# FFN norms of an attention and FFN megakernel: squares added up on VectorE in fp32, fewer statistic matmuls, and the closing 1/sqrt by Ln and Exp

## The reference

```python
def attn(X):                                     # layer 0, attention
    q, k, v = X@Wq.T + bq, X@Wk.T + bk, X@Wv.T + bv
    s = where(j > i, -inf, einsum('bie,bje->bij', q, k) / sqrt(E))
    return softmax(s, axis=-2) @ v
def ffn(x):                                      # three blocks
    h = x
    for blk in range(3):
        y = qlora_linear(h, 2*blk)               # w = q/7.5 - 1, times scale; plus a rank-32 term and a bias
        y = (y - mean(y)) * rsqrt(var(y) + 1e-5) * gamma + beta
        y = gelu(y)
        h = qlora_linear(y, 2*blk + 1) + h
    return h
x = layernorm(X + attn(X))
out = layernorm(x + ffn(x))
```

## Time and profile before

| | us |
|---|---|
| median of 3 runs | 1446.7 (1445.36 to 1462.48) |
| the profiled execution | 1443.28 |
| its span, slowest core (5) | 1441.7 (cores: 1429.3 to 1441.7) |
| TensorE busy | 1339.1 (93%) |
| VectorE busy | 698.4 (48%) |
| ScalarE busy | 750.5 (52%) |
| GpSimd busy | 424.5 (29%) |
| table loads on ScalarE | 48 of 1.283 each |

### The profile page before, as it was taken

The page is one execution under the profiler, slowest core; times in us unless marked ns, Lnnn a source line. Parts: engine busy times, 40 slices in busy tenths (PEclk is TensorE's granted clock), DMA queues, the critical chain, the costliest instruction groups (busy, mean ns, idle before and its releaser), DMA issues.

```text
span 1441.7 us, 21149 instructions; the slowest of 8 cores (1429.3 to 1441.7 us)
## 1 busy us (share of the span) xinstructions
PE 1339.1 (93%) x6724; PEld 620.1 (43%) x6724; DVE 698.4 (48%) x1474; ACT 750.5 (52%) x1104; POOL 424.5 (29%) x308
## 2 busy tenths in 40 slices
PE   6979999969899999888999999999989999999994
PEld 2434444434344444443444444445534444444552
DVE  1225555433344354416464365468634624736774
ACT  0135226653213356422784686576668748847741
POOL 4022353786623256654000019100100000650010
PEclk9988999989999999989999999999999999999998
DMA  9956545686855343485011035215641010550022
GB/s 137 217 164 201 172 146 139 198 239 204 282 177 203 117 147 131 167 292 224 11 59 46 14 104 169 78 32 190 222 143 58 2 59 1 182 169 1 30 103 103
DMA packets 70699, 192.17 MB, mean 133 GB/s; under 512 B 5696, under 2 KB 16192, under 8 KB 67520
## 3 DMA queue, kind: packets, MB, share of 16 engines
q1 hardware_dynamic: 48192, 133.40, 28.5%
q0 software_dynamic: 22400, 57.42, 14.3%
HBM read 158.03 MB, written 46.14 MB: 142 GB/s over the span
## 4 chain that ended last, share of the span: by engine, by line
PE 79%; DVE 5%; POOL 5%; issue 4%; ACT 3%; DMA 2%; another core or an unknown queue 1%; DVEq 0%; SPq 0%; ACTq 0%; POOLq 0%
PE ps L212 79%; ACT POOLT L216 3%; DVE POOLT L220 2%; POOL POOLT L612 2%; POOL POOLT L652 2%; DMA POOLT<-wq 1%; POOL POOLT L102 1%; DVE SM L994 1%; DMA POOLT<-bv_h 1%; DVE SM L229 1%; DVE POOLT L226 0%; POOL POOLT L394 0%; DVEq L108 0%; DVE POOLT L721 0%
## 5 line engine op out<-in xcount | busy, mean ns | idle before, releaser
L212 PE MATMUL ps<-POOLT 128*128 128x512 bf16 (+2 forms) x5600 | 1262.0, 378 | 30.7 <-DMA POOLT<-lb_h 8.7
L212 PEld LDWEIGHTS ps<-POOLT 128*128 128x128 bf16 (+1 forms) x5600 | 540.2, 99 | 685.1 <-issue 113.0
L216 ACT ACTIVATE POOLT<-ps,SM 128x512 bf16<-128x512 f32 (+4 forms) x396 | 262.6, 683 | 258.7 <-PE ps L212 156.5
L220 DVE TENSOR_TENSOR POOLT<-POOLT 128x512 bf16<-128x512 bf16 (+1 forms) x448 | 254.4, 604 | 211.9 <-ACT POOLT L216 191.6
L216 ACT ACTIVATE POOLT<-POOLT 128x512 bf16<-128x512 f32 (+4 forms) x234 | 175.8, 762 | 228.0 <-DMA POOLT<-qw_t 83.6
L220 DVE TENSOR_TENSOR POOLT<-ps,POOLT 128x512 bf16<-128x512 f32 (+1 forms) x176 | 117.0, 688 | 177.0 <-PE ps L212 151.9
L952 POOL TENSOR_TENSOR POOLT<-POOLT 128x512 f32<-128x512 f32 x64 | 89.6, 1424 | 373.8 <-DMA POOLT<-x1s 366.2
L394 POOL TENSOR_TENSOR POOLT<-POOLT 128x1024 f32<-128x1024 f32 x48 | 112.7, 2348 | 275.2 <-DMA POOLT<-sc_t 131.5
L216 ACT ACTIVATE POOLT<-POOLT,CF 128x512 bf16<-128x512 bf16 x192 | 154.3, 808 | 26.4 <-DVE POOLT L220 25.6
L212 PE MATMUL ps<-POOLT,CB 128*128 128x512 bf16 x320 | 116.5, 394 | 47.6 <-ACT POOLT L216 38.3
L216 ACT ACTIVATE POOLT<-POOLT,SM 128x512 bf16<-128x512 f32 (+2 forms) x120 | 110.0, 918 | 78.3 <-DVE SM L223 43.1
(11 more groups left out here) (53 smaller groups left out, 303.8 us busy)
## 6 DMA issues: line engine op xcount, KB each, us to landing
POOLT<-qw_t SPq DMA_DIRECT2D x48, 512.0 KB, 4.2
POOLT<-sc_t SPq DMA_DIRECT2D x48, 512.0 KB, 5.5
POOLT<-weffs SPq DMA_DIRECT2D x24, 1024.0 KB, 7.8
POOLT<-xt SPq DMA_DIRECT2D x16, 1024.0 KB, 10.6
x1s<-POOLT POOLq DMA_DIRECT2D x16, 1024.0 KB, 5.4
POOLT<-x1s SPq DMA_DIRECT2D x8, 2048.0 KB, 10.9
POOLT<-x1s SPq DMA_DIRECT2D x64, 256.0 KB, 3.2
out<-POOLT POOLq DMA_DIRECT2D x28, 512.0 KB, 4.1
```

Source lines behind the costliest of these rows:

```text
L212: return pe.put(lambda e: e.matmul(out, lhsT, rhs, start=start, stop=stop), *after, sig=sig)
L216: return act.put(lambda e: e.activation(out, in_, func, bias=bias, scale=scale, accum_out=acc), *after)
L220: return dve.put(lambda e: e.tensor_tensor(out, a, b, op), *after)
```

## The change

In y1 a chunk is still squared on VectorE, but into fp32, and the squares of a norm are added up there in fp32; only the last addition writes bf16, and one statistic matmul takes that sum (blocks 0 and 1). In the last block sums of two chunks are taken, so four statistic matmuls a norm. `add_square` replaces the square and the call of `after_groups(3, ...)`; it uses `after_groups(2, ...)`. The rates of `pre` in y1 go from 0.75 to 0.5. Ln and Exp on ScalarE with two waits replace the first 12 operations of a closing. Buffers are laid out anew for this.

```diff
+F_RS = (A_P2, A_MU, A_RS, A_SQ)
+F_TMP = (A_P2 + 512, A_P2 + 1024)
+F_SQ = A_P2 + 1536
+F_ACC = (A_LORA, A_LORA + 512)
...
+        def add_square(t, n, o, ty, stat_mm):
+            i = cnt["acc"] % 2
+            per = 8 if n < 2 else 2
+            k = o % per
+            tmp = FTMP[o % 2]
+            if k == 0:
+                sums[i] = v_tt(FACC[i], FY[t][o], FY[t][o], ALU.mult, ty, p_att)
+                return
+            ts = v_tt(tmp, FY[t][o], FY[t][o], ALU.mult, ty, p_att)
+            if k < per - 1:
+                sums[i] = v_tt(FACC[i], FACC[i], tmp, ALU.add, ts, sums[i])
+                return
+            q = cnt["sq"] % 3
+            cnt["sq"] += 1
+            cnt["acc"] += 1
+            tq = v_tt(FSQ[q], FACC[i], tmp, ALU.add, ts, sums[i], fsq_free[q])
+            after_groups(2, lambda: stat_mm(o, q, tq))
...
             for o in range(EC):
-                pre(0.75, 0.75)
+                pre(0.5, 0.5)
...
-                q = cnt["sq"] % 5
-                cnt["sq"] += 1
-                tq = v_tt(FSQ[q], FY[t][o], FY[t][o], ALU.mult, ty, fsq_free[q])
+                add_square(t, n, o, ty, stat_mm)
                 post()
-                after_groups(3, lambda o=o, q=q, tq=tq: stat_mm(o, q, tq))
...
-                ve, y, a, c2, nm = (two(x) for x in (28, 30, 32, 34, 36))
-                t1 = v_ts1(ve, var, EPS, ALU.add, *tb)
-                yi, vi = smi[:, fo + 30:fo + 30 + np_], smi[:, fo + 28:fo + 28 + np_]
-                t1 = v_ts1(yi, vi, 1, ALU.logical_shift_right, t1)
-                t1 = v_ts(yi, yi, -1, 0x5f3759df, ALU.mult, ALU.add, t1)
-                for _ in range(3):
-                    t1 = v_stt(a, y, -0.5, y, ALU.mult, ALU.mult, t1)
-                    t1 = v_tt(c2, a, ve, ALU.mult, t1)
-                    t1 = v_stt(y, c2, 1.5, y, ALU.add, ALU.mult, t1)
+                y, nm = two(30), two(36)
+                t1 = a_act(y, var, AF.Ln, *tb, bias=col(S_EPS))
+                t1 = a_act(y, y, AF.Exp, t1, scale=-0.5)
                 t1 = v_stt(nm, mean, -1.0, y, ALU.mult, ALU.mult, t1)
```

More of the change, by code:

```diff
@@ L702, in build_program @@
         FRS = [f32v(a, 512) for a in F_RS]
-        FSQ = [b16v(F_SQ + s * 256, 512) for s in range(5)]
+        FSQ = [b16v(F_SQ + s * 256, 512) for s in range(3)]
+        FACC = [f32v(a, 512) for a in F_ACC]
+        FTMP = [f32v(a, 512) for a in F_TMP]
         FXR = [f32v(F_XR + s * 512, 512) for s in range(4)]
@@ L833, in build_program @@
         fy_free[2], fy_free[3] = (p_att,), (p_att,)
-        frs_free = [(p_att,)] * 4
-        fsq_free = [p_att] * 5
+        frs_free = [(p_att,), None, None, None]
+        fsq_free = [p_att] * 3
         act_att = (act.sem, act.n)
-        cnt = {"sq": 0, "rs": 0, "xr": 0, "out": 0, "fo": 0}
+        cnt = {"sq": 0, "rs": 0, "xr": 0, "out": 0, "fo": 0, "acc": 0}
+        g0 = [0]
         finals = []
@@ L858, in post @@
                 gel_now.pop(0)()
+        sums = [None, None]
+        def add_square(t, n, o, ty, stat_mm):
[15 more added lines that the diff above has]
+            after_groups(2, lambda: stat_mm(o, q, tq))
         def y1(t, n):
@@ L866, in stat_mm @@
             def stat_mm(o, q, tok):
-                if o == 0:
+                if sb[0] is None:
                     sb[0], fr = bank_take()
+                    first = True
                 else:
-                    fr = ()
-                p = mm(ps[sb[0]][:], ones_b, FSQ[q], o == 0, o == EC - 1, tok, *fr, sig=True)
+                    fr, first = (), False
+                p = mm(ps[sb[0]][:], ones_b, FSQ[q], first, o == EC - 1, tok, *fr, sig=True)
                 fsq_free[q] = p
@@ L903, in y1 @@
                            *(fr if c == 0 else ()), sig=c == EC - 1)
-                late = sq_free if (cnt["sq"] == 4) else ()
+                late = sq_free if (g0[0] == 0 and n == 0 and t == 0 and o == 4) else ()
                 ty = a_act(FY[t][o], ps[b][:], AF.Identity, p, k_fb,
@@ L1048, in build_program @@
         for g in range(NSEQ):
+            g0[0] = g
             for n in range(NBLK):
@@ L1063, in build_program @@
                             pieces.pop(0)()
+                        frs_free[1:] = [(*rs_free, *mu_free, *sq_free)] * 3
                         xr_free = [(rg_free[1],)] * 4
```

3 lines of the change are left out of this document (removed).

## The result

The changed kernel takes 1492.95 us (median of 4 runs, 1491.6 to 1494.48), the kernel before beside it 1446.0 (median of 4); the ratio is 1.0324, interval 1.0288 to 1.0361. It is slower by 47 us. The forecast was 1464 with a range of 1424 to 1480. The profiled execution's slowest core spans 1492.2 us, 50.5 more than before.

The account below looks back on a forecast made before the run. TensorE, busy 93% of the span, was taken as the bound: 57.2 us removed against 74.3 added, net +17.1, plus 2 for the clock on 1443.3 gave 1462.4, with half the run offset 1464 us; range 1424 to 1480.

Parts of the forecast that it names:

- The likeliest case: Whole kernel: removed work is outweighed by late statistic matmuls, giving 1464 us; chance 0.48.
- the other tiles of the first two blocks: First two blocks, tiles 1 to 3: statistic matmuls late by 2.3 us at tile 1, 3.5 at tiles 2 and 3.
- removed steps 1 to 3: Savings: 144 statistic matmuls 31.1 us, 16 waits on VectorE 11.7, the wait at the second sequence's start 5.8.
- step 2: FFN: TensorE's 16 waits on VectorE before statistic matmuls go, 11.7 us saved.
- The chain of 2.74 us: Group's end to statistic matmul: start of square, fp32 square, add and hops take 2.74 us, 1.01 late.
- The ring: First two blocks, tiles 1 to 3: copy, square, add, rescale, gelu, copy take 3.83 us per two groups, against 3.45.
- steps 4 and 5: New closing: y3's waits on banks shrink, 4 us saved (0 to 7.5); the tail's last two closings save 4.6.
- Tile 0 has no gelus beside it: 1.01.: First two blocks, tile 0: only the short chain counts, so each statistic matmul is 1.01 us late.
- With the first statistic matmul after 9 groups nothing waits there.: Start of second sequence: the 3.90 us wait goes, with the clock loss behind it, 5.8 us saved.
- the possible 13.6: Clock: eight waits above 2.47 us could each cost about 1.7 us at 1.2 GHz; only 2 us taken.
- the third rival's mechanism: Slower, 1478 us: waits of 3.5 us throw TensorE to 1.2 GHz each time, 13.6 us, y3 gains nothing; chance 0.20.
- Some 0.8 for the copies behind table loads: Last block: some 0.8 us added to 32 late statistic matmuls at 1.01 each, 33.1 us together.

Follow-up runs that it names:

- number 7: Changed kernel with squares and sums kept in bf16 instead of fp32, same slack: 1458.1 us; cores 4 to 7 0.997 of the kernel before.
- number 6: Changed kernel with each y1 gelu queued on ScalarE behind the next group's copy: 1490.4 us; cores 4 to 7 1.022 of the kernel before.
- number 4: Kernel before with only the rates of pre in y1 changed from 0.75 to 0.5: 1448.2 us, ratio 1.0011.
- number 3: Kernel before with only the closing changed, to Ln and Exp on ScalarE: 1431.5 us, ratio 0.9892.
- Numbers 9 and 10: Two variants of the changed kernel: first tile's statistic matmuls 8 groups behind, ratio 1.0306; GpSimd's last four multiplications left out, ratio 1.0273.
- number 2: Changed kernel with four groups of slack instead of two in after_groups, in the last block alone: 1473.3 us, ratio 1.0186.
- numbers 8 and 12: Changed kernel with bf16 sums over 8 chunks everywhere, statistic matmuls 4 groups behind (6 in very first tile), rates 0.75: 1435.8 us; measured again 1414.8 us, ratio 0.9781.

## Why the prediction was wrong

The likeliest case had the right sign and, in most of its terms, the right places; 1464 against 1493 comes mostly from three steps that failed, and for the rest from one term that was sized too small. Measured against the profiled executions, in us:

| step of the prediction | forecast | measured | difference |
|---|---|---|---|
| first tile, first sequence | 1.0 | 10.8 | +9.8 |
| first tile, second sequence | 1.0 | 4.4 | +3.4 |
| the other tiles of the first two blocks | 39.2 | 41.0 | +1.8 |
| last blocks | 33.1 | 37.6 | +4.5 |
| the clock | 2 | 14.7 | +12.7 |
| y3, saved | 4 | 2.8 | +1.2 |
| tail, saved | 4.6 | 6.8 | -2.2 |
| sum, with the removed steps 1 to 3 as forecast | net 19.1 | 50.3 | +31.2 |

The spans differ by 50.5, so little is left open, though rows of this kind agree so closely partly by luck.

**What was right.** The 144 matmuls went; the 16 VectorE waits of step 2 went with them. The chain of 2.74 us against 1.73 of slack was right to 0.01 where nothing else stood in it: forecast 1.01 late, read 0.86 and priced 1.02; with bf16 the forecast of the same sum was met too (number 7). The ring was right in kind and size: for the twelve tiles behind the first ones, where the short chain alone would have given 12 x 1.01, and the ring 37.2, TensorE waited 38.8. By single tiles the agreement is in part luck: the second and third tile of a middle block were forecast at 2.3 and 3.5 and cost 3.6 and 2.8, since each fall of the clock took some 1 us off the next wait. When the ring was opened (number 6), the waits fell to the 2 us that had been worked out. The rule of the Trainium skill on 16-bit operands (VectorE: DVE Perf Modes, "What auto-detection actually checks"), under which the square stands at the upper price, is what the trace shows: 0.69 with an fp32 result, 0.42 with all in bf16. The other one (ScalarE: Activation LUTs, "What ACT_TABLE_LOAD costs": 2.66 us a switch) is again not: load at 822.52, gelu at 823.82, 1.30 later. The rates were worth nothing (number 4, in the kernel before; in the changed one they weren't tried by themselves), and the 8.6 us for the closing in steps 4 and 5 were if anything too small (number 3: 15 us in the kernel before, with what it gains at the second sequence's start).

**Failed step: "Tile 0 has no gelus beside it: 1.01."** TensorE waited 10.8 us there in place of 1.0. I looked at what TensorE and ScalarE do there and not at VectorE's queue, which at the first tile holds four casts of x1 and runs beside GpSimd's last multiplications. The sign stood in the trace of before, in lines of its timeline that I had not looked at. Three squares took 5.39 us beside two multiplications on GpSimd, the first two 2.58 and 2.56 and the third, when GpSimd was done, 0.41; the next one took 5.09 instead of 0.43:

```profile
670.49 5.25 POOL L652 TENSOR_TENSOR POOLT<-POOLT 128x1024 f32<-128x1024 f32 x2 [16.00 <-ACT POOLT L216]
670.96 5.39 DVE L220 TENSOR_TENSOR POOLT<-POOLT 128x512 bf16<-128x512 bf16 x3
676.74 5.09 DVE L220 TENSOR_TENSOR POOLT<-POOLT 128x512 bf16<-128x512 bf16 x1 [0.39 <-ACT POOLT L216]
```

Before, VectorE had one operation a group and could be held up without harm; the longest wait it caused was 1.77. After, it has two, and what it can't win back lands on TensorE. Numbers 9 and 10 tell the two explanations apart: more slack only moves the wait, taking the GpSimd work away removes it.

**Failed step: "With the first statistic matmul after 9 groups nothing waits there."** The wait of 3.90 did go, and one of 4.25 stands in its place. It had covered something that stood right behind it, the casts of the next tile's x1. Before:

```profile
1041.82 0.32 SPq L102 DMA_DIRECT2D POOLT<-x1s  x1
...
1054.36 1.05 ACT L216 ACTIVATE POOLT<-POOLT 128x1024 bf16<-128x1024 f32 x1
```

The load was issued at 1041.82 and ScalarE came to the first of these casts 12.5 us later, held up with TensorE; it didn't have to wait. After, the load is issued at 1076.84 and ScalarE has its last copy done at 1084.45, 7.6 us later, while the cast can start only 11.7 us behind the issue, at 1088.51. What it would take to issue that load earlier was not tried.

**Failed step: "since a slow TensorE also lets the ring catch up I take 2 us of the possible 13.6."** The full 13.6 was the right size (14.7 in 9 falls). A slow TensorE does let the ring catch up: after the fall behind 690.22 the next wait is 2.56, after a tile at full speed it is 3.66, and so at the other tiles. But this is a trade of about 1 us of wait for 1.6 of clock, not a gift, and I had counted the gain without the cost. This was the third rival's mechanism, at 0.20; it should have been part of the likeliest case, because that case itself forecast eight waits above the length at which before's rows show a fall.

**Mis-sized term: the last block.** "Some 0.8 for the copies behind table loads" was counted once for all; six of the eight tiles pay 0.9 to 1.3 us more than the regular wait for it (1.75 to 2.12 against 0.86), and the two waits of 1.01 a little; the two last waits, 0.41 and 0.42, give 0.9 back.

Steps 4 and 5 together were off by one microsecond, in opposite directions. The forecast that y3 loses nothing more held only because the last block waited: without those waits (number 2) y3 waited 11.5 us more.

## What to carry to other kernels

Moving a reduction from an engine that is full to one that is half idle pays only if the result is due later than the longer chain takes: write down the slack in front of the consumer (here one group, 1.73 us) and the chain (2.74 with fp32, 2.2 with bf16), and if it doesn't fit, give it more slack in the same edit and look where the backlog lands next (numbers 8 and 12 did so, and are faster than the kernel before). Count an engine's load in the stretch where it is fullest, with the durations that operations have there, beside the neighbours that slow them, and not with the mean. When waits are added in front of TensorE, add the clock to their price: here 9 of the 16 above 2 us cost 1.3 to 1.7 us more each.

## What was not expected of the hardware

VectorE and GpSimd hold each other up, and not in proportion: where a VectorE operation with all its data in SBUF meets a GpSimd multiplication of 128x1024 fp32, one of the two, mostly VectorE's, ends only behind the other. In the kernel before, squares of 0.43 took 2.58, 2.56 and 5.09 us and ended 0.3 behind the multiplication; the last of them was held through two in a row (676.89 to 681.54). After, a cast took 3.37 instead of 1.22, a square 2.83 and an addition 5.71 instead of 0.69, and the square and the addition ended 0.55 behind. GpSimd's pair took 6.19 where it met the two casts, and 4.65 where it met the addition, which did all the waiting. At 642.80 in the changed kernel a pair took 4.67 beside two VectorE additions that read one input from PSUM, and these took 0.69 each: none was held up.

Not every long wait costs clock. Between tiles of the changed kernel the wait of 10.65 was followed by 1.6 us lost and the one of 2.56 behind it by none, though 3.66 behind that was again. A wait of 2.17 (at 744.48) was followed by a loss of 1.7, one of 3.44 (at 1132.47) by none. I can say what a fall costs (1.3 to 1.7 us) but not which of the waits between 2.1 and 3.6 brings one.
